# High half of up's first weights by GpSimd instead of ScalarE in the prologue of a cross-attention and mixture-of-experts kernel

## What is computed

```python
x = x + xattn(layernorm(x), ctx, ctx, Wq, bq, Wk, bk, Wv, bv)      # softmax(q k^T / sqrt(128)) v
h = layernorm(x)
probs = softmax(einsum('bsh,eh->bse', h, router_w))
a_h = gelu(einsum('bsh,ah->bsa', h, actor_w1) + actor_b1)
actor_logits = clip(einsum('bsa,ka->bsk', a_h, actor_w2) + actor_b2, -30, 30)
sampled_k = argmax(actor_logits) + 1
scores = where(rank(probs) < sampled_k, probs, 0)
for e in range(8):
    g, u = einsum('bsh,ih->bsi', h, gate_w[e]), einsum('bsh,ih->bsi', h, up_w[e])
    out = out + scores[..., e:e+1] * einsum('bsi,hi->bsh', silu(g) * u, down_w[e])
x = x + out
```

## Time and profile before

| | us |
|---|---|
| median of 3 runs | 748.61 |
| lowest and highest | 748.22, 748.76 |
| the profiled execution, its own time | 748.52 |
| its span in the trace | 746.6 |
| TensorE busy | 735.6 (99%) |
| VectorE, ScalarE, GpSimd busy | 636.9, 558.2, 589.4 |

### The profile page before, as it was taken

How to read it: one execution, slowest core, us unless ns; L and a number is a source line. 1 busy time by engine, 2 the same in 40 slices (tenths; PEclk the granted TensorE clock), 3 DMA queues, 4 the chain that set the end, 5 groups by cost and what they waited for, 6 DMA issues and landing times.

```text
span 746.6 us, 13864 instructions
## 1 busy us (share of the span) xinstructions
PE 735.6 (99%) x3680; PEld 363.5 (49%) x3680; DVE 636.9 (85%) x1407; ACT 558.2 (75%) x990; POOL 589.4 (79%) x630
## 2 busy tenths in 40 slices
PE   7999999999999999999999999999999999999998
PEld 5544454544545445454544545445454544444445
DVE  7899888897889889888897989889888897878777
ACT  5998787776877777777776877777777776877664
POOL 2686979799796987979689796987979688687763
PEclk9999999999999999999999999999999999999999
DMA  9200412214043252323423243242333323120110
GB/s 352 73 16 1 83 31 54 47 28 94 15 104 70 58 98 56 97 55 86 81 50 96 54 105 69 57 96 55 97 55 86 69 51 76 35 51 14 30 28 29
DMA packets 128511, 50.49 MB, mean 68 GB/s; under 512 B 106832, under 2 KB 117072, under 8 KB 128464
## 3 DMA queue, kind: packets, MB, share of 16 engines
q1 hardware_dynamic: 128032, 49.47, 27.9%
q10 hardware_dynamic: 432, 0.48, 0.2%
HBM read 28.92 MB, written 13.40 MB: 57 GB/s over the span
## 4 chain that ended last, share of the span: by engine, by line
PE 93%; DVE 3%; ACT 2%; issue 1%; DMA 0%; POOL 0%; DVEq 0%; POOLq 0%; ACTq 0%
PE bank L690 29%; PE bank L691 28%; PE bank L692 28%; PE bank L586 2%; PE bank L557 2%; PE bank L651 1%; PE bank L670 1%; PE bank L594 1%; PE bank L593 1%; PE bank L595 1%; DVE bank L1661 0%; DMA x_in<-in_x 0%; ACT up_hi L885 0%; DVE hid_lo L1667 0%; DVE w_abs L1346 0%
## 5 line engine op out<-in xcount | busy, mean ns | idle before, releaser
L1286 POOL TENSOR_TENSOR weighted<-silu,score_bc 128x512 f32<-128x512 f32 x336 | 430.4, 1295 | 86.7 <-ACT silu L1037 82.8
L1661 DVE SCALAR_TENSOR_TENSOR bank<-bank,h_scale,weighted 128x512 f32<-128x512 f32 x336 | 253.4, 754 | 83.7 <-PE bank L692 68.2
L1031 ACT ACTIVATE hid_hi<-bank 128x512 f16<-128x512 f32 x336 | 200.7, 597 | 147.7 <-DVE bank L1661 145.6
L1037 ACT ACTIVATE silu<-bank,silu_scale 128x512 f32<-128x512 f32 x336 | 230.5, 686 | 24.0 <-PE bank L692 23.8
L1667 DVE TENSOR_TENSOR hid_lo<-bank,hid_hi 128x512 f16<-128x512 f32 x336 | 227.5, 677 | 0.0
L690 PE MATMUL bank<-xn_lo,gate_hi 128*128 128x512 f16 x336 | 127.6, 380 | 2.0 <-ACT silu L1037 2.0
L690 PE MATMUL bank<-xn_lo,up_hi 128*128 128x512 f16 x336 | 127.4, 379 | 1.2 <-DVE hid_lo L1667 0.9
L692 PE MATMUL bank<-xn_hi,up_hi 128*128 128x512 f16 x336 | 127.4, 379 | 0.0
L691 PE MATMUL bank<-xn_hi,up_lo 128*128 128x512 f16 x336 | 127.4, 379 | 0.0
L692 PE MATMUL bank<-xn_hi,gate_hi 128*128 128x512 f16 x336 | 127.3, 379 | 0.0
L691 PE MATMUL bank<-xn_hi,gate_lo 128*128 128x512 f16 x336 | 127.3, 379 | 0.0
(11 more groups left out here) (220 smaller groups left out, 809.6 us busy)
## 6 DMA issues: line engine op xcount, KB each, us to landing
x_in<-in_x SPq DMA_DIRECT2D x16, 256.0 KB, 2.7
y_kept<-y_sb SPq DMA_DIRECT2D x60, 64.0 KB, 2.6
y_tok<-y_kept SPq DMA_DIRECT2D x15, 256.0 KB, 2.8
out<-out_sb SPq DMA_DIRECT2D x15, 256.0 KB, 2.1
xt_in<-in_x_t SPq DMA_DIRECT2D x14, 256.0 KB, 2.9
row_bc<-row_kept SPq DMA_DIRECT2D x14, 256.0 KB, 4.2
ctx_in<-in_ctx_t SPq DMA_DIRECT2D x14, 240.0 KB, 2.9
v_kept<-raw_gate SPq DMA_DIRECT2D x10, 256.0 KB, 2.0
```

The costliest lines, as they stand in the source:

```text
L1031: af(hid_hi[j % HRING][:], up_bank[j % U_BANKS][:], ACT.Copy).then_inc(hid_hi_ready, 1)
L1037: af(silu[j % RING][:], gate_bank[(par + j) % G_BANKS][:], ACT.Silu, scale=silu_scale[:])\
L1286: g.tensor_tensor(weighted[j % RING][:], silu[j % RING][:], score_bc[par][:], ALU.mult)\
L1661: v.scalar_tensor_tensor(up_bank[j % U_BANKS][:], up_bank[j % U_BANKS][:], h_scale[:], weighted[j % RING][:], ALU.mult, ALU.mult).then_inc ...
```

## The change

One call leaves ScalarE's prologue and a call of the same work enters GpSimd's, behind gate's high half and ahead of `route_probs(0)`. GpSimd's product has two operands (the raw weights and `w_mul` spread over the columns) where ScalarE's was a copy with a scale.

```diff
@@ scalar, prologue
             keys(4, up_bank[0])
             exps(1)
-            weight_high(1)
             router_exps(0)
             nc.scalar.preload_act_table(ACT.Silu)
@@ gpsimd, prologue
             weight_high(0, 0, FIRST_TILES)
             x2_low(0, 0)
             weight_high(0, FIRST_TILES, PART)
+            weight_high(1, 0, PART)
             route_probs(0)
             rank_over(0)
```

## The result

| | before | after |
|---|---|---|
| median of 22 runs each, us | 748.52 | 749.38 |
| lowest and highest, us | 748.19, 750.57 | 749.07, 754.12 |
| runs between 753.7 and 754.2 us | 0 | 5 |
| profiled execution, its span, us | 748.52, 746.6 | 749.48, 747.7 |

The ratio after to before, in which all runs count and which is not that of the medians, is 1.0025, with a 95% interval from 1.0016 to 1.0033: the changed kernel is slower. Two things lie in this number. The median rose by 0.86 us (0.11%), near the 0.92 of the forecast's sum, and 5 of 22 runs, all at 753.71 to 754.12 us, pull the ratio over 0.2%. The forecast had a case at that time, and gave it one chance in 25. The mean granted TensorE clock of a whole execution was 0.995 in each of these 5 runs and 0.999 or 1.00 in the other 17, the common runs.

What follows compares the result with a forecast made beforehand. TensorE's work was taken as the bound, so a prologue shift reaches the end whole: VectorE's 1.18 us delay less 0.26 from the removal gives 0.92, 748.52 + 0.92 = 749.44, stated as 749.5 us; range 748.3 to 750.1.

Steps and rivals of the forecast that it cites:

- the forecast's sum: Router's chain in the prologue: VectorE 1.18 us later, less 0.26 from the removal, makes exponentials and end 0.92 us later.
- a case at that time: TensorE's clock falling behind its longer prologue wait: +4 us, 753.5 us; chance 0.04.
- What bounds the kernel, and the shift that reaches the end whole: TensorE is busy almost throughout from 43.3 us, so a shift of the transposes at 29.81 us reaches the end whole.
- The removal is worth 0.26 us at most: ScalarE's 1.04 us copy holds the router's exponentials only from 25.94 to 26.20 us, so removing it brings at most 0.26.
- what the removal gives back: The 0.26 us that the sum subtracted from VectorE's 1.18 us delay for ScalarE's removed copy.
- The length of the added product, 1.68 us: GpSimd's 896-column product of up, from 24.36 to 26.04 us, priced at 0.61 us plus 640 columns at 1.67 ns.
- VectorE stands for the whole product: VectorE's low half of gate's 640 columns, issued under GpSimd's product, waits for its end: near 2.06 us instead of 0.88.
- The exponentials, probabilities and transposes 0.92 us later: Router's chain keeps its distances: exponentials at 27.12 instead of 26.20 us, transposes at 30.73 instead of 29.81.
- Rival 3, TensorE's clock: Clock falls to 1.2 GHz behind TensorE's gap grown to about 1.9 us: +4 us, 753.5 us; chance 0.04.
- Rivals 1 and 2: VectorE's low half under GpSimd's product: 1, not held, 748.3 us, chance 0.06; 2, both share, 748.5 us, chance 0.08.

Runs made afterwards that it cites:

- the removal alone: Changed kernel with GpSimd making only 32 of up's 896 columns and ScalarE's copy still gone: 748.20 us median of 11, beside 748.50 for the kernel before.
- the addition alone: Kernel before, ScalarE's copy kept, plus GpSimd's 896-column product into a free tile: 4 of 12 runs at 749.27 to 749.33 us, 8 at 753.71 to 753.96.
- the product made twice: Changed kernel with GpSimd's product made a second time into a free tile: 4 of 6 runs at 754.23 to 754.44 us, the others 749.62 and 750.26.

## Why the prediction was right in its sum and wrong in its chances

- **What bounds the kernel, and the shift that reaches the end whole**: right. Down's first matmul came 0.92 us later (1.08 less the 0.16 of the load), the median 0.86 (0.79 without the 5 runs near 754).
- **The removal is worth 0.26 us at most**: right, 0.27 in the trace of the removal alone (0.30 between the medians). But the words "what the removal gives back" were loose: in the changed kernel it gives back nothing, since with the addition alone the common time is the same. The 0.26 us are slack that the delay of VectorE used up first.
- **The length of the added product, 1.68 us**: 1.67 measured, so the correction of the disturbed 1.44 us row was needed; the straight line through the raw rows would have given 1.99. The estimate of 1.87 us by the 2.5 cycles an element of the Trainium skill, GPSIMD Engine Reference, section 2.1, came out 0.20 too long: the measured 1.67 us decides for this product, in which one operand is a single column spread over all.
- **VectorE stands for the whole product**: right: the low half took 2.05 us (2.06 forecast) and ended 0.69 us behind it (0.69). Writing instead of reading made it vanish, and the issue order turned round made it vanish.
- **The exponentials, probabilities and transposes 0.92 us later**: 27.24, 27.99 and 30.87 us, less 0.16 each 27.08, 27.83 and 30.71, against 27.12, 27.85 and 30.73.
- **Rival 3, TensorE's clock**: its mechanism and its place were right. Its price was near by luck in part: it forecast +4 us and 753.5 from 4.2 us of work at half speed, a length for which it gave no row; the clock was low for 6.8 us and cost 3.0, and waits behind it cost another 1.4, which gives 753.9. Its chance, 0.04, is the step that failed. It rested on "No gap of the trace brought a fall", and with that on one profiled execution and on gaps of 0.96 us at most, while the change was to make one of 1.86. The trace of before could not bear out so small a chance for a wait twice as long as any that it shows. In 17 of 44 runs of the changed kernel and of the addition alone, which have this wait, the clock fell for the long time. Left out of the sum, the fall was worth 5 / 22 x 4.5 = 1.0 us in the mean of the changed kernel's 22 runs, about as much as the shift that the sum held.
- So the median, 749.38, lies where the sum put it (749.44), but 5 of 22 runs lie 4.5 us above, the ratio is 1.0025, and "slower by over 0.2%" is what the comparison shows, to which the forecast gave 0.08.
- Rivals 1 and 2 are out: a free or a shared overlap would have left the low half under 1.3 us.

## What to carry to other kernels

Work moved onto an idle stretch of GpSimd is free for GpSimd's queue only; look which VectorE instructions with two SBUF operands are issued under it, because in every such pair measured here the later one stood until the earlier one was all but done, and a small delay enters whatever chain it carries. Price a longer TensorE wait twice, once as a shift and once as a fall of the clock behind it that occurs in a part of the runs; here the first was 0.8 to 0.9 us and the second 1.0 in the mean. A profile of one execution cannot show how often such a thing happens: time the kernel often enough to see the second group.

## What the runs showed of the hardware that was not expected

- The same program with the same waits ran with the granted clock at 1.00 throughout, or (in the profile of the addition alone) at 0.50 from 30.4 to 37.2 us: 17 of 44 runs near 754 us, all 17 with a mean clock of 0.995, for a wait of 1.87 us followed by three matmuls and a wait of 0.44. The shares differed between groups (5 of 22, 8 of 12, 4 of 10), which the runs don't explain.
- The clock fell for a shorter time in one execution with waits of 0.70 and 1.04 us, from 30.8 to 34.25 us; that run was 1.6 us slower than its kernel's median. Such short falls (mean clock 0.998) occur in the kernel before, too, with waits of 0.96 and 0.44 us, in 5 of 91 runs.
- A waiting VectorE instruction got its turn between two GpSimd products that followed each other without a gap: it ended 0.67 us behind the first, and the second took 2.26 us instead of 1.68 (the product made twice).
